# A depthwise-convolution kernel: the banded filter matrices laid out with the horizontal shift outermost and their high and low parts side by side

## What is computed

```python
def _gn(v, G=32, eps=1e-05):               # mean and variance over 6 channels x 56 x 56
    ...
x = x + conv(_gn(x), L0_conv_weight, groups=192, padding=15) + bias      # 31 x 31 taps
kernels = hat_functions(weight_coord, radius) @ weights                  # 11 x 11 taps
x = x + conv(_gn(x), kernels, groups=192, padding=5)
```

## Time and profile before

| | us |
|---|---|
| median of 2 runs | 4035.39 (4034.21 to 4036.58) |
| span of the profiled execution, first to last instruction | 4033.4 |
| PE busy, weight loads busy | 3843.8, 3814.6 |
| DVE busy | 3376.0 |
| POOL busy | 2161.0 |
| ACT busy | 1006.1 |
| first matmul starts at | 51.98 |

### The profile page before, as it was taken

The page is one execution under the profiler, slowest core; times in us unless marked ns, Lnnn a source line. Parts: engine busy times, 40 slices in busy tenths (PEclk is TensorE's granted clock), DMA queues, the critical chain, the costliest instruction groups (busy, mean ns, idle before and its releaser), DMA issues.

```text
span 4033.4 us, 60018 instructions
## 1 busy us (share of the span) xinstructions
PE 3843.8 (95%) x19008; PEld 3814.6 (95%) x19008; DVE 3376.0 (84%) x5047; ACT 1006.1 (25%) x1618; POOL 2161.0 (54%) x1545
## 2 busy tenths in 40 slices
PE   4899999999999999999999999999999999999996
PEld 4899999999999999999999999999999999999996
DVE  8888888888888888888888888888888888888876
ACT  1222222222222222222222222222222222222222
POOL 4355555555555555555555555555555555555555
PEclk9999999999999999999999999999999999999998
DMA  6766655556554656555566646565556665465542
GB/s 177 183 144 136 140 132 127 136 124 153 128 139 117 139 134 142 130 133 131 128 148 137 136 116 142 126 147 128 136 126 137 143 140 132 118 141 121 131 106 62
DMA packets 121670, 539.03 MB, mean 134 GB/s; under 512 B 28250, under 2 KB 43738, under 8 KB 99610
## 3 DMA queue, kind: packets, MB, share of 16 engines
q1 hardware_dynamic: 121498, 537.50, 57.7%
HBM read 449.06 MB, written 88.33 MB: 133 GB/s over the span
## 4 chain that ended last, share of the span: by engine, by line
PE 73%; DVE 14%; issue 7%; POOL 3%; DMA 1%; ACT 1%; SPq 0%; DVEq 0%; POOLq 0%; ACTq 0%
PE acc L860 73%; DVE x_lo L681 3%; DVE halves L621 2%; POOL yt L486 2%; DVE raw L704 2%; DVE yt L689 1%; DVE scratch L668 1%; DMA toep<-padded 1%; DVE raw L707 1%; POOL p L489 1%; DVE part L656 1%; DVE norm L649 0%; ACT p L547 0%; SPq L367 0%; DVE scratch L696 0%
## 5 line engine op out<-in xcount | busy, mean ns | idle before, releaser
L860 PE MATMUL acc<-x_hi,toep 128*112 128x448 f32 (+4 forms) x12672 | 3601.0, 365 | 177.5 <-DVE x_lo L681 102.5
L860 PEld LDWEIGHTS acc<-x_hi,toep 128*112 128x112 f32 x12672 | 3052.4, 280 | 203.0 <-issue 153.6
L860 PE MATMUL acc<-x_lo,toep 128*112 128x448 f32 (+4 forms) x6336 | 2304.6, 364 | 0.0
L860 PEld LDWEIGHTS acc<-x_lo,toep 128*112 128x112 f32 x6336 | 1772.1, 280 | 3.4
L486 POOL TENSOR_TENSOR yt<-p 128x448 f32<-128x448 f32 x384 | 608.8, 1585 | 1146.7 <-ACT p L547 1110.6
L506 POOL TENSOR_TENSOR x_lo<-xs,x_hi 128x480 fp32r<-128x480 f32 x384 | 577.6, 1504 | 347.3 <-ACT x_hi L538 345.1
L499 POOL TENSOR_TENSOR xs<-xt 128x480 f32<-128x480 f32 x384 | 470.2, 1224 | 337.1 <-DVE xt L674 337.1
L536 ACT ACTIVATE x_hi<-xt 128x960 fp32r<-128x960 f32 x384 | 387.2, 1008 | 928.1 <-DVE xt L674 928.1
L689 DVE TENSOR_TENSOR yt<-acc,p 128x448 f32<-128x448 f32 x384 | 236.6, 616 | 446.3 <-PE acc L860 329.0
L696 DVE STREAM_TRANSPOSE scratch<-yt 128x896 f32<-128x896 f32 x384 | 556.4, 1449 | 22.7 <-DVE yt L689 11.6
L681 DVE TENSOR_TENSOR x_lo<-xt,x_hi 128x960 fp32r<-128x960 f32 x384 | 524.8, 1367 | 2.1 <-ACT x_hi L536 2.1
(11 more groups left out here) (53 smaller groups left out, 309.1 us busy)
## 6 DMA issues: line engine op xcount, KB each, us to landing
toep<-padded SPq DMA_DIRECT2D x192, 552.0 KB
toep<-padded SPq DMA_DIRECT2D x192, 468.0 KB
toep<-padded SPq DMA_DIRECT2D x192, 372.0 KB
raw<-in_x_dram SPq DMA_DIRECT2D x96, 672.0 KB, 13.0
out_dram<-raw SPq DMA_DIRECT2D x192, 336.0 KB, 7.7
toep<-padded SPq DMA_DIRECT2D x384, 117.0 KB
toep<-padded SPq DMA_DIRECT2D x192, 138.0 KB
toep<-padded SPq DMA_DIRECT2D x192, 94.5 KB
```

Source lines behind the costliest of these rows:

```text
L860: last = nc.tensor.matmul(dst, toeplitz(toep, f, place, part, k), src[:, h, cols], start=(m == 0 and part == 0 and src is x_hi), stop=(m = ...
```

## The change

The order of the numbers becomes: shift, image row, output parity, part. The four numbers of one image row at one shift (`cell = 4`) are output parity x part, so that high and low part stand side by side. All image rows of one shift are a `slab` of 56 cells. The matrix of one shift and part is now read with a step of 2 numbers where it was 48 (`f1`) or 18 (`f2`). In DRAM the slabs of a filter share their zero margins, so one filter and input parity has 4476 numbers (`f1`) or 996 (`f2`), where it had 5856 and 1476.

A load of a band is no longer one run for each partition, but one run for each partition and shift: `(hi - lo) * 4` numbers, which are 496, 736, 624 and 368 bytes for `f1` and 336, 416, 416 and 208 bytes for `f2`. It takes two DMAs, one for each column parity of the input (every second partition). Work areas move as the sizes want. No compute instruction is added or removed; `padded_rows` now has its innermost dimension in steps of a whole slab.

```diff
-        self.half = 2 * self.L
-        self.row = 2 * self.half
-        self.block = H * self.row
+        self.cell = 4
+        self.slab = H * self.cell
+        self.block = self.L * self.slab
...
-        self.rows = K + 2 * self.margin
-        self.padded = self.rows * self.row
-        self.pitch = (self.rows - self.margin) * self.row
+        self.period = (K + self.margin) * self.cell
+        self.padded = self.L * self.period + self.margin * self.cell
...
         def padded_rows(f, place, part):
-            rows = padded(f, place).rearrange("p (r o e m) -> p r o e m", o=2, e=2, m=f.L)
-            return rows[:, f.margin:f.margin + f.K, :, part, :]
+            rows = padded(f, place)[:, 0:f.L * f.period].rearrange("p (m r o e) -> p e r o m", m=f.L, o=2, e=2)
+            return rows[:, part, f.margin:f.margin + f.K, :, :]
...
-                    src = bass.AP(padded, m * (2 * f.padded) + (lo - HB * q + f.pad + first) * f.row,
-                                  [[f.row, rows], [f.padded, 2], [1, (hi - lo) * f.row]])
-                    sp.dma_start(toep[2 * (HB * q + first):2 * HB * (q + 1), place, lo * f.row:hi * f.row].bitcast(F32), src
-                                 ).then_inc(landed[place], 16)
+                    for e in range(2):
+                        src = bass.AP(padded, m * (2 * f.padded) + e * f.padded + (lo - HB * q + f.pad + first) * f.cell,
+                                      [[f.cell, rows], [f.period, f.L], [1, (hi - lo) * f.cell]])
+                        slabs = toep[2 * (HB * q + first) + e:2 * HB * (q + 1):2, place, :].rearrange(
+                            "p (k n) -> p k n", n=f.slab)
+                        sp.dma_start(slabs[:, :, lo * f.cell:hi * f.cell].bitcast(F32), src).then_inc(landed[place], 16)
...
-                return bass.AP(toep, place * f.block + part * f.L + k, [[T_RING * f.block, P], [f.half, M]])
+                return bass.AP(toep, place * f.block + k * f.slab + part, [[T_RING * f.block, P], [2, M]])
...
-                    pe.wait_ge(landed[c % T_RING], g * (16 * BANDS * CG // T_RING) + 16 * BANDS * (c // T_RING + 1))
+                    pe.wait_ge(landed[c % T_RING], g * (16 * 2 * BANDS * CG // T_RING) + 16 * 2 * BANDS * (c // T_RING + 1))
```

More of the change, by code:

```diff
@@ L288, in conv_norm_kernel @@
         spare = raw[0:CP, 1:X_RING, :].rearrange("p g n -> p (g n)")
-        area_size = f1.pitch + f1.padded
+        area_size = max(2 * f1.padded, CG * RUN + 4 * f2.padded)
         area = spare[:, 0:area_size]
@@ L304, in padded @@
         def padded(f, place):
-            start = 0 if f is f1 else area_size - (3 * f2.pitch + f2.padded)
-            return area[:, start + place * f.pitch:start + place * f.pitch + f.padded]
+            start = 0 if f is f1 else area_size - 4 * f2.padded
+            return area[:, start + place * f.padded:start + (place + 1) * f.padded]
         def padded_rows(f, place, part):
-            rows = padded(f, place).rearrange("p (r o e m) -> p r o e m", o=2, e=2, m=f.L)
-            return rows[:, f.margin:f.margin + f.K, :, part, :]
+            rows = padded(f, place)[:, 0:f.L * f.period].rearrange("p (m r o e) -> p e r o m", m=f.L, o=2, e=2)
+            return rows[:, part, f.margin:f.margin + f.K, :, :]
         STAGES = [[(f1, 0, 0)], [(f1, 1, 0)], [(f2, 0, 0), (f2, 1, 2)]]
@@ L754, in filters_low @@
                 if k == 2:
-                    step(nc.vector.memset(area[:, area_size - (3 * f2.pitch + f2.padded):], 0.0))
+                    step(nc.vector.memset(area[:, area_size - 4 * f2.padded:], 0.0))
                     step(nc.vector.memset(spare[:, work_start:work_start + 2 * work_size], 0.0))
```

## The result

The changed kernel takes 3867.24 us (median of 2 runs, 3866.96 to 3867.53), 168 us less than before. The ratio is 0.9583, with a 95% interval of 0.9555 to 0.9611. The forecast was 3891 us.

A forecast was written before the change was run, and what follows sets the result against it. PE was taken to bound most of the time, with DVE setting the pace for 34 us behind slot 7. 4033.4 - 150 (faster matmuls) + 6 (start) = 3889, plus 2 us around the span: 3891 us, range 3690 to 4060.

The forecast's parts named there:

- The stationary matrix: PE's matmuls in slots 0 to 7: faster matrix reads save 4.85 us a round, 150 us over 31 rounds.
- The middle value: PE's matmul times, between no change and losing both costs: 203, 189, 176 and 163 ns at 448, 416, 384, 352 columns.
- the floor of 192 ns: Least time of a PE matmul however few its columns, laid to the stationary matrix load; forecast to go.
- the 16 ns above the columns: What a PE matmul takes beyond streaming its columns, seen at 448 columns; forecast to stay.
- The 34 us behind slot 7 are DVE's and stay.: From the end of slot 7 to the next slot 0 DVE sets the pace; those 34 us were to stay.
- DVE is ready for it.: DVE's waits for PE in slots 3, 5, 7, 9.5 us together, let the 4.85 us through; none gets to zero.
- The start: Before the first matmul: strided layout writes +4 us, store and added load issues +2 us, together 6 us later.
- DMA: Matrix loads in short runs: 14 ns a run, 3.7 us more per job pair, 16.3 against 19.6 us, hidden; share about 75%.
- SP: SP's queue: eight DMA issues a job take about 6 us, with input and output 79 of 118 us; not on the path.
- the 16 ns go too: Rival on PE's matmuls: the extra above the columns also vanishes; DVE's bound 3700 us, taken as 3750 us; chance 0.18.
- the floor is not the step: Rival on PE's matrix load: 32-bit numbers load slowly at any step, nothing gained, 4041 up to 4060 us; chance 0.28.
- the DMA engines become the bound: Rival on matrix loads: at 40 ns a run PE waits for `toep`, 540 us more, 4570 us; chance 0.17.

The follow-up runs named there:

- the first experiment: Kernel before the change, old layout and loads, with only the stationary matrix's read step set to 2 numbers (wrong products, same work): 3900.09 us, ratio 0.9659.
- two products: Changed kernel without the product of the high matrix with x_lo, so one matmul in three is left out: 3867.86 us, run once.

## Why the prediction held, and where it was off

- **The stationary matrix.** The middle value was right: the floor of 192 ns went and the 16 ns above the columns stayed. It was a choice between two bounds, with no row of a small step behind it. Forecast were 203, 189, 176, 163 ns, measured 203, 190, 176, 161. An F job lost 1.02 us (14.14 to 13.11, forecast 0.94). The S job lost 0.25 us (5.62 to 5.37) where 0.05 was forecast: its three matmuls of 480 columns, which the sum left out, went from 708 to 654 ns together, the fifteen of 448 from 207 to 203 each, the nine of 416 from 200 to 190. With that, 5 x 1.02 + 3 x 0.25 = 5.85 us, of which slots 0 to 7 show 5.25 on average (88.34 to 83.09 us from slot 0 to slot 8). In 7 of 30 rounds PE now waits ahead of slot 3 (0.28 us over all rounds), and slot 0 has the lower clock more often.
- **"The 34 us behind slot 7 are DVE's and stay."** Nearly: 34.56 to 33.74 us, which is 24 us over 29 rounds. The waits for POOL that stood in DVE's way, 3.1 us a round, are gone, and most of that is eaten by the slower residual sums (L708 from 1.65 to 2.05 us on average).
- **DVE is ready for it.** Right in sum: its waits for PE fell by 4.4 us a round. But not evenly: over 30 rounds the wait in slot 1 went from 1.0 to 0.1 us, in slot 3 from 2.7 to 0.9 (to nothing in 12 rounds, where the prediction said that none would), in slot 5 from 2.2 to 1.3, in slot 7 from 4.6 to 3.8.
- **The start.** Mis-sized: some 14 us against 6 (6.5 ahead of the first round, and the first round is 9.9 us over the mean of the others, before 2.0), and 20 us with the step of before. Three steps of it failed. It read the copies' 4.08 us as the price of a step; they take 0.87 us elsewhere in the same trace and stood beside POOL's zero fill. It put the later stages of filters under PE's first jobs; PE waits 7.60 us for DVE ahead of the fourth job. And it counted SP's added issues only ahead of the first matmul, within 2 us; PE waits for matrices in the first round too, and 4.6 us longer in the last six S jobs, which were to "count as unchanged". The old layout with twice the DMAs shows the same two losses.
- **DMA.** 14 ns a run were too much. Summed over the packets of the trace, a run of 736 bytes takes 64 ns and one of 208 bytes 22 ns, and the matrix loads keep an engine for 2031 us in place of 1677, which is 8.5 ns for each of the additional runs (354 us x 16 engines / 666,624 runs), some 2.1 us for a pair on the busiest engine and not 3.7. The share is 71.9% in the loop and not 75%. Hidden, as said. The Trainium skill's page "DMA: Bandwidth & Descriptors" (section "Specifications") gives 512 bytes as the least transfer for full rate. No jump is seen there in these runs: one of 496 bytes takes 36 ns and one of 624 bytes 55. Further below a byte costs somewhat more (208 bytes in 22 ns).
- **SP.** 6.12 us for eight, as forecast.
- **The rival "the 16 ns go too".** Wrong in its mechanism, and its price was wrong as well. It took 3700 us as DVE's bound, by subtracting DVE's waits from the round. With two thirds of PE's work gone the time is 3832 us. A wait that is taken away was not idle time to be had: with it gone DVE's own instructions got longer, and so did its waits of the kind "issue".
- **The rival "the floor is not the step"** falls with the first experiment, "the DMA engines become the bound" with a share of 71.9% and no wait of PE for a matrix in the loop. The queue that does become a bound is SP's, which the prediction had weighed only at its present size.

On the rule of the Trainium skill's page "SBUF — State Buffer" (section "Door 1: The DMA port swizzle"), that full bandwidth wants at least two hits in a line of 16 bytes: the loads agree with it, at 182 ns with step 2 and 280 with 48. Step 3, with one or two hits in a line, lies between at 231 ns. That step 4 is slower than 48 does not follow from it. No step reached the prediction's estimate of 93 ns for a load (174 at step 1); the floor went all the same at 182 ns, above the 161 ns of 352 columns, as the estimate of 88 ns above has it.

**Luck in the sum.** The forecast gain of the span, 144 us, is 24 us short of the measured one, but that is two misses against each other. The 30 rounds behind the first gave 181.6 us, 36 us more than forecast: 24 of them come from the stretch behind slot 7, which was to stay, the others from F and S jobs. The start, the first round and the end took back 12.9 us, 12 us more than forecast.

## What to carry over

Where matmuls with fewer columns are no faster than those with more, look at the load of the stationary matrix, and read it with a step of one or two 32-bit numbers; time the smaller step in the old layout first, whatever it then reads, before anything is rebuilt. When the layout is paid for with more and shorter transfers, count what their issuing engine spends on each (0.8 us here) before the bytes, in the first round and at the end as well as in the loop. And do not take "round minus waits" as the bound of the next engine: take work away from the first one and measure.

## What had not been expected of the hardware

- A load of 128 x 112 numbers of 32 bits took 174, 182, 231, 293 and 280 ns at steps of 1, 2, 3, 4 and 48 (18 in S jobs). It showed in the distance of the matmuls only from step 4 on.
- DVE stood up to 5.1 us at one instruction with long runs (up to 17,664 bytes, 1.37 us on an engine) on the DMA engines, and each such wait over 1 us ended 1.4 to 1.8 us behind an 8 KB packet of instructions; with the transfers cut in two the waits were 2.5 us at most and the kernel 33 us faster. Waits as long came with short runs too (5.6 us with two products).
- Gaps of 2.30 us on PE (median) were followed in every other round by 3.4 us at 1.2 GHz, gaps of 2.57 us in 18 of 30; those of 1.38 and 0.53 us in none.
- DVE's residual sum L704 over 896 numbers took 1.12 to 1.16 us with POOL idle and 2.02 to 2.07 us beside POOL's work, in the same kernel.
- Twice as many runs of half the length kept a DMA engine for 1797 us in all and not 2031, where the issuing queue left the engines half idle.
